# A transformer block in fp32: next batch's x loaded tile by tile, and its statistics, low halves and value tile at other places among the heads

## What is computed

```python
xn = layernorm(x)                                   # over the 512 features
q, k, v = xn @ Wq + bq, xn @ Wk + bk, xn @ Wv + bv  # 16 heads of 32
scores = q @ k.T / sqrt(32) + alibi_slope[head] * (key - 511)   # causal mask
ctx = softmax(scores) @ v
gate_w, up_w, down_w = cubic splines through control points, 2048 x 512 each
ffn = (silu(xn @ gate_w.T) * (xn @ up_w.T)) @ down_w.T
out = x + ctx @ Wo + bo + ffn
```

## Time and profile before

| what | value |
|---|---|
| runs | 773.27, 775.70, 783.23 us; median 775.7 |
| profiled execution | 774.91 us, span of its trace 773.1 us |
| PE busy | 679.8 us, 88% of the span |
| DVE busy | 457.9 us, 59% |
| ACT busy | 445.4 us, 58% |
| POOL busy | 330.7 us, 43% |
| mean granted clock of PE | 0.971 |
| moved by DMA | 109.75 MB |

### The profile page before, as it was taken

How to read it: one execution, slowest core, us unless ns; L and a number is a source line. 1 busy time by engine, 2 the same in 40 slices (tenths; PEclk the granted TensorE clock), 3 DMA queues, 4 the chain that set the end, 5 groups by cost and what they waited for, 6 DMA issues and landing times.

```text
span 773.1 us, 13681 instructions
## 1 busy us (share of the span) xinstructions
PE 679.8 (88%) x4884; PEld 543.3 (70%) x4884; DVE 457.9 (59%) x1290; ACT 445.4 (58%) x705; POOL 330.7 (43%) x191
## 2 busy tenths in 40 slices
PE   4978779989789898799898777788979999999997
PEld 3756657777567776578776565566758888888885
DVE  6287867879857878768799686665323213223122
ACT  4388867877857878677879663444322333232331
POOL 1565554555535545444546430322125236335334
PEclk9998999999899999999999999899989999999999
DMA  7986377475765375672946937859248475243101
GB/s 246 163 184 119 54 225 134 62 135 158 125 163 82 43 123 111 138 150 42 206 82 96 365 109 256 269 134 281 60 141 253 129 233 179 88 121 126 39 1 54
DMA packets 53067, 109.75 MB, mean 142 GB/s; under 512 B 6408, under 2 KB 6664, under 8 KB 51464
## 3 DMA queue, kind: packets, MB, share of 16 engines
q1 hardware_dynamic: 51416, 106.46, 56.1%
q10 hardware_dynamic: 1584, 2.43, 1.2%
HBM read 59.32 MB, written 25.17 MB: 109 GB/s over the span
## 4 chain that ended last, share of the span: by engine, by line
PE 39%; DVE 5%; issue 4%; POOL 3%; ACT 3%; DMA 2%; ACTq 1%; SPq 0%; POOLq 0%; DVEq 0%
PE bank L1471 6%; PE bank L1472 6%; PE bank L1473 6%; PE bank L1458 3%; PE bank L1459 3%; PE bank L583 2%; PE bank L638 2%; PE bank L585 2%; POOL resid L1625 2%; PE bank L584 2%; DMA bm_early<-bases_scratch 2%; PE bank L624 1%; DVE w_new L1569 1%; ACTq L365 1%; ACT w_new L1509 1%
## 5 line engine op out<-in xcount | busy, mean ns | idle before, releaser
L1153 POOL TENSOR_TENSOR work<-work 128x1280 f16<-128x1280 f32 x64 | 171.1, 2673 | 176.5 <-ACT work L1050 176.5
L1617 POOL TENSOR_TENSOR in_lo<-inner,in_hi 128x512 fp32r<-128x512 f32 x64 | 85.2, 1333 | 202.8 <-ACT in_hi L1535 202.8
L830 DVE CUSTOM_DVE_ANT_0 work<-bank,dist 128x128 f32<-128x128 f32 (+3 forms) x256 | 115.4, 487 | 78.8 <-PE bank L624 61.7
L1042 ACT ACTIVATE work<-work,neg_max 128x128 f32<-128x128 f32 (+3 forms) x256 | 130.1, 562 | 18.4 <-DVE neg_max L830 18.2
L1535 ACT CAST in_hi<-inner 128x512 fp32r<-128x512 f32 x64 | 39.8, 622 | 147.1 <-PE bank L1473 141.1
L1581 DVE TENSOR_TENSOR inner<-bank,silu 128x512 f32<-128x512 f32 x64 | 44.1, 689 | 132.5 <-ACT silu L1529 125.1
L638 PE MATMUL bank<-ident,work 128*128 128x128 f16 x1280 | 105.2, 226 | 10.3 <-DVE work L839 8.3
L1050 ACT CAST work<-work 128x1280 f16<-128x1280 f32 x64 | 80.7, 1260 | 55.3 <-PE bank L638 54.7
L638 PEld LDWEIGHTS bank<-ident,work 128*128 128x128 f16 x1280 | 75.4, 101 | 46.8 <-issue 33.3
L1471 PE MATMUL bank<-w_room,in_hi 128*128 128x512 f32 x256 | 101.4, 396 | 0.5 <-POOL in_lo L1617 0.5
L1472 PE MATMUL bank<-w_room,in_hi 128*128 128x512 f32 x256 | 101.0, 395 | 0.0
(11 more groups left out here) (100 smaller groups left out, 1300.7 us busy)
## 6 DMA issues: line engine op xcount, KB each, us to landing
q_stack<-parts SPq DMA_DIRECT2D x48, 256.0 KB, 5.7
k_stack<-parts SPq DMA_DIRECT2D x48, 256.0 KB, 6.1
z<-xt_scratch SPq DMA_DIRECT2D x128, 88.0 KB
x_in<-x SPq DMA_DIRECT2D x32, 256.0 KB, 4.1
xt_scratch<-xt_room SPq DMA_DIRECT2D x8, 1024.0 KB, 6.7
xt_room<-xt_scratch SPq DMA_DIRECT2D x6, 1024.0 KB, 9.9
factor<-c_basis SPq DMA_DIRECT2D x5, 1024.0 KB, 9.3
taps<-windows SPq DMA_DIRECT2D x5, 1024.0 KB, 11.1
```

Of the source, the lines that this page charges most:

```text
L830: dve.tensor_tensor_reduce(probs[:, s % 2, OFF[i]:OFF[i] + n], score_bank[i % 2][:, 0:n], dist[:, S - n:S], -slope(s), 3.4e38, ALU.add, AL ...
L1042: e = act.activation(tile, tile, ACT.Exp, bias=neg_max[:, s % 2, i:i + 1], scale=-1.0)
L1153: pool.tensor_tensor(probs16[:, s % 2, 1, :], probs[:, s % 2, :], probs16[:, s % 2, 0, :], ALU.subtract).then_inc(lo_ready, 1)
L1617: pool.tensor_tensor(in_lo[k % 2][:, :], inner[:, k % 2, :], in_hi[:, k % 2, :].bitcast(F32), ALU.subtract).then_inc(il_ready, 1)
```

## The change

Five edits, all for the next batch's x.

1. SP: x tiles 0 and 1 are loaded as soon as their own sums are stored, ahead of the store of the fourth sum; tiles 2 and 3 follow behind it (`room_for_x`). For batch 1 the loads stay where they were.
2. DVE: the statistics of tiles 0 and 1 are taken at the end of step 7, those of tiles 2 and 3 at the end of step 8.
3. POOL: the two powers go to the start of steps 8 and 9.
4. DVE: the low halves of x tiles 2 and 3 stand in step 11 between score tiles 1 and 2, no longer at the step's end.
5. DVE: the sum of value tile 0 stands at the end of step 11, no longer in step 12.

```diff
@@ attention_vector, step @@
-                if kind == "v":
+                if kind == "v" and n > 0:
                     v_take(of, n)
                 elif kind == "o" and n > 0:
                     add_residual(of, n)
+            if s == 11:
+                for of, (_, n) in turns:
+                    x_low(of, n)
             if s < H:
                 bias_and_max(b, s, (2, 3))
...
-            for of, (kind, n) in turns if s != 3 else []:
+            for of, (kind, n) in turns if s not in (3, 11) else []:
                 (x_low if kind == "x" else ctx_low)(of, n)
             if carry and s == 3:
                 add_residual(b - 1, 0)
-            if carry and s in (8, 9):
-                norm_stats(b + 1, (2 * s - 16, 2 * s - 15))
+            if s == HALF - 1 and b < B - 1:
+                norm_stats(b + 1, (0, 1))
+            if carry and s == HALF:
+                norm_stats(b + 1, (2, 3))
+            if carry and s == 11:
+                v_take(b + 1, 0)
@@ attention_gpsimd, step @@
-            if carry and s in (9, 10):
-                inverse_std(b + 1, s - 9)
+            if carry and s in (8, 9):
+                inverse_std(b + 1, s - 8)
@@ attention_sync @@
+        def room_for_x(b, q):
+            sp.wait_ge(res_st[q], 16 * b)
+            sp.nop(nofuse=True)
+            if b < B - 1:
+                load_x(b + 1, q)
...
+        for t in range(QT):
+            load_x(1, t)
         for b in range(1, B):
-            for t in range(QT):
-                load_x(b, t)
             stack(b - 1, 3)
...
-            for q in range(1, QT):
-                store_sum(b - 1, q)
-            for q in range(QT):
-                sp.wait_ge(res_st[q], 16 * b)
-            sp.nop(nofuse=True)
+            store_sum(b - 1, 1)
+            store_sum(b - 1, 2)
+            room_for_x(b, 0)
+            room_for_x(b, 1)
+            store_sum(b - 1, 3)
+            room_for_x(b, 2)
+            room_for_x(b, 3)
```

## The result

The changed kernel takes 771.4 us (median of 20 runs, 765.11 to 779.57), the kernel before 776.7 beside it (20 runs, 771.58 to 783.56). The ratio, which leaves out executions over 1.5% above the fastest of their kernel, is 0.9937, interval 0.991 to 0.9964: by it 4.9 us less, between 2.8 and 7.0; the two medians differ by 5.4. The forecast was 6.4 us less. The profiled execution took 770.4 us, its span is 768.6 for 773.1.

The account below looks back on a forecast made before the run. PE was taken to bound steps with projections, DVE steps 8 to 10. Terms: 0.42 - 2.57 = -2.15 us a carry, three carries -6.4, from 775.7 to 769.3 us; range 768 to 771 (0.50), eight in ten 764.5 to 777.5.

Parts of the forecast that it names:

- The late edits: Steps 11 and 12: PE's waits before q0 and k0 vanish, gaining 1.49 + 1.08 = 2.57 us a carry.
- The low halves hidden: Step 11: 1.28 us of low halves fits DVE's 1.37 us wait for score tile 2, 0.09 to spare.
- Rival B: Step 11: low halves aren't hidden, at worst 1.28 us a carry come back, 773.1 us; chance 0.10.
- The statistics in steps 7 and 8: DVE starts step 8 1.80 us later; 0.68 lies under slack, so steps 8 and 9 run 1.12 us late.
- The return in step 10: Step 9 loses one statistics pair, so 0.70 us is recovered: from step 10 on 1.12 - 0.70 = 0.42 us late.
- Rival D: Steps 8 to 10: PE's clock falls to 1.2 GHz, +4.8 us a carry, 790; chance 0.08 together with late x loads.
- rival A: Step 9: POOL's instruction goes before DVE's second normalization, about 2.45 us later a carry, 776.6 us; chance 0.22.
- The loads of x: Batches 2 and 3: x tiles 0 and 1 land in time, cost 0, at worst 3 us a carry in two carries.
- The sum: All three carries: 0.42 - 2.57 = -2.15 us each, -6.4 us in all, forecast 769.3 us.

Follow-up runs that it names:

- the run with both obstacles removed: Changed kernel plus POOL's wait for both normalizations in step 10 and unused matmuls on PE in steps 8 and 9: 765.8 us, ratio 0.9862.

## Why the prediction was right, and where it wasn't

The sign and the range held, and 4.9 us against 6.4 is near, but in part by luck. The parts were further off than the sum, and their errors partly cancelled: a carry got 0.4 us more from the late edits than forecast, lost 0.2 more to the early statistics, and got nothing of the 0.70 back. Carries 2 and 3 are shorter by 1.6 and 2.0 us for a forecast of 2.15, and the first is longer by 1.6.

- **The late edits.** Forecast 1.49 + 1.08 = 2.57 us a carry, measured 1.67 + 1.27 = 2.94. The place was right, the size was short, because I took the idle time as the whole price. Without a wait PE also begins the next matmul before the modelled end of the one ahead: q0 starts at 112.58, while the transposes of 111.81 last 0.95 us, to 112.76. That 0.18 us comes on top of each wait: 1.49 + 0.18 = 1.67, 1.08 + 0.18 = 1.26. PE was full behind it, and the gain was kept.
- **The low halves hidden.** Forecast 0.09 us to spare, measured 0.17 us of DVE's wait left. Rival B didn't happen.
- **The statistics in steps 7 and 8.** Forecast 1.12 us late, measured 1.74 - 0.41 = 1.33 in carries 2 and 3, and 0.98 in the first, whose step 7 was longer before. PE's wait at score tile 2 was 0.89.
- **The return in step 10.** This is the step that failed: "1.12 - 0.70". It came nowhere in the changed kernel: steps 9 and 10 together were 14.1 and 14.0 us in carries 2 and 3, for 14.1 and 14.3 (where the third had lost 0.74 us to POOL before), and 17.1 for 13.6 in the first. Its size was right, 0.65 us in the run with both obstacles removed, and in one carry of the run in which POOL waits. What I hadn't carried through is that it hangs on the clock at which PE turns x: the forecast took the 0.70 from a carry at the full clock, and the changed kernel turned x at the lower one in carries 2 and 3. Rival D had the cause and a price for a much longer stretch; a step 9 at the lower clock is 0.9 us longer than one at the full clock (7.37 for 6.47).
- **POOL between the normalizations (rival A).** It came in the first carry, at about its price: forecast 2.45 us, step 9 was 10.07 for 7.36 and 7.37 in the other two, 2.7. It came by another way than forecast. The prediction had POOL early, at 94.57, 4.76 us into the step, and that is to the hundredth where POOL stands in all three carries when PE is kept busy; so the near tie (94.57 against 94.70) goes to POOL at the full clock. With the lower clock it stands at 5.5 and DVE wins, as the prediction had it "against" this rival. In the first carry of the changed kernel POOL was late too, at 5.59, but DVE was later, for its product had lost to the qk low half by 0.02 us. By the Trainium skill ("SBUF — State Buffer", Who interferes with whom) the loser waits out the other's whole instruction; the pair of 3.33 us beside POOL's 2.61 agrees.
- **The loads of x.** No statistics waited for a DMA: step 7 of carries 2 and 3 grew by 1.74 us, within 0.1 of the 1.80 that the statistics take, and by the same in the run without the late edits.
- **The sum.** In the two traces the carries differ by 2.0 us, not by 6.4 nor by the 4.9 of the ratio. The other 2.5 of the 4.5 us between the spans lie where nothing was changed: 0.5 ahead of step 7 of the first carry, 0.6 in the last batch, 1.5 from the start of its last head to the end of the program. These parts scatter from execution to execution: over the nine kernels profiled here step 7 begins between 75.70 and 78.65 us, and the part from the last head's start on takes 320.1 to 325.9. How often POOL gets in over the 20 timed runs was not measured. If it did so in no carry, the steps would give about 4.7 us (134.18 less 132.20, plus 2.7), which is near the ratio's 4.9; that is argued, not shown.

The half of the change that gives it its name costs more than it returns. Even with both obstacles removed a carry takes 41.9 us, for 41.3 in the two carries of the late edits alone, with the same added matmuls, whose clock stayed up. The two moves at its end are worth the rest.

## What to carry to other kernels

Price each part of a combined change by the lengths of the steps that it touches, and run the parts alone: here two small moves were worth 7.9 us in the carries, and the larger part took 6.0 of that back, 2.7 of it where POOL got in (by the medians, 5.7 of 11.1). Work moved out of a full stretch pays only if the engine that is waited for next can use the room; look at that engine's order, its clock after the idle time, and who takes a shared resource once a wait in front of it is gone. When removing one obstacle makes things worse, try it together with the next one before giving up the theory.

## What was not expected

- A wait removed ahead of a PE matmul gave 0.18 us more than the idle time in the profile, twice per carry.
- In step 9 DVE's product of 0.29 us usually starts 0.1 us ahead of POOL's qk low half. Starting 0.02 us behind it led to the 2.7 us that the first carry of the changed kernel lost.
- The faster PE made the kernel slower: with unused matmuls in the waits, step 9 went from 7.36 to 8.74 us in the second carry, because ACT and then POOL came earlier and POOL's 2.6 us instruction got ahead of DVE's 0.5 us one.
- Filling PE's waits kept the clock full until x was turned in step 9, but not always behind it: in the last carry of the late edits with added matmuls it fell over steps 10 and 11 and made step 11 1.05 us longer (9.89 for 8.84); in the run with both removed it fell in none of these steps.
